# Neighbourhood attention on one core: values written to DRAM by SP's queue, scores and values interleaved in sets of three

## The chip, the cores and the metric

One Trainium2 chip, one of its cores. The engines are TensorE (PE; PEld is its weight load), VectorE (DVE), ScalarE (ACT), GpSimd (POOL) and SyncE (SP), each with its own instruction queue; SP computes nothing, it issues most of the DMAs. The metric is the device time of one execution in microseconds; all times below are microseconds. The kernel before took 715.81 in the median of three runs (713.94 to 717.45).

## The reference

Two blocks on an image batch x of shape 2 x 48 x 48 x 384, each with a group norm in front and a residual around it. The first, which the change touches, is 7 x 7 neighbourhood attention with 16 register tokens:

```python
qkv = gn(x) @ qkv_w.T + qkv_b                      # 12 heads of 32
reg_kv = registers @ qkv_w[384:].T + qkv_b[384:]   # 16 keys and values seen by every query
scores = einsum('bnqe,bnke->bnqk', q, concat(k, reg_k)) / sqrt(32)
scores = where(in_7x7_window_or_register, scores, -1e30)
o = einsum('bnqk,bnke->bnqe', softmax(scores), concat(v, reg_v))
x = x + o @ out_w.T + out_b
```

The second is a mixture of 4 experts, 2 of them chosen per token, of width 96. Matrix products are made in three float16 passes (high x high, high x low, low x high).

## The kernel before

There are six attention **stages** (`gi` 0 to 5): image `gi // 3`, and 4 of the 12 heads (128 channels). A stage works on six vertical **strips** of 8 columns by 48 rows (`s`, 384 tokens). Within a strip there are six **slots** of eight rows (`a`), so 36 steps n = 6s + a. Each stage has three parts.

*Opening.* Keys of the stage (six row blocks), which ScalarE and VectorE split into halves and SP writes to the DRAM scratch `kscr`; then per strip the queries, written to `qscr` by POOL (`queries_out`, L332), between them the output projection of the stage before (`project_out`, added into X by VectorE at L517). In stages 2 and 5, after the projection, `parameters` (VectorE) and `deviation` (ScalarE, with a change of activation table on each side) make the next group norm's scale, and TensorE waits for it (`gn_par`) before its next work. In stage 0 `value_bias` stands between the queries of strips 4 and 5, and TensorE waits for its result `obx` (L593) before the scores.

*Middle part.* It makes two things. First, the **scores for maxima** of strips 0, 1 and 2: `scores(gi, s, i)`, six units i of eight matmuls (L1002) each, each unit in one PSUM bank, each reduced by VectorE (`maximum`, L523). When the six are done, `split_maxima` splits them, `maxima_turned` on TensorE transposes them (L1012), ScalarE copies them (`maxima_out`, L776, semaphore `t_ev`), and POOL sends them into two rows of QS by DMA (`maxima_in`, L355). Second, the **values** of all six strips: `values(gi, s, b)`, 27 matmuls a strip, three for each of three channel blocks and three token blocks b, into the bank `V_BANK`. ScalarE copies a strip to `VT[:, s % 2]` (`values_out`, L770, semaphore `v_sb`). POOL writes it with three DMAs to `vscr` (`values_out`, L339, semaphores `v_out[s % 2]`). VT has two buffers, so ScalarE's copy of strip s waits until the write of strip s - 2 has landed. SP loads windows of `vscr` into VR (`values_in`, L255: six DMAs a strip, 14 columns of a slot each, semaphores `vr_in`), which waits for the writes of strips s and s + 1.

TensorE's order is: scores 0 (six units), values 0, values 1, turn maxima 0, scores 1, values 2, values 3, turn maxima 1, scores 2, values 4, values 5. ScalarE's: values 0, 1, maxima 0, values 2, 3, maxima 1, values 4, 5. POOL's: values 0, 1, register values, maxima 0, values 2, 3, maxima 1, values 4, 5.

*Steps.* 36 steps: `key_scores(gi, n)` (L1026, transposed scores less the maxima), ScalarE's exponentials (`exps`, L787, four buffers), and `weighted(gi, n)` (L1045, weighted values and sums), issued two steps behind. The scores of strips 3, 4 and 5 for their maxima are spread between them. `weighted(gi, 0)` waits for the first three transfers of VR. The scores of strip 4 stand behind step 13 and wait for its keys in the slot of strip 0 (`kb_in`).

**SP's queue** sets much of the order. For each stage, in program order:

```python
for s in range(4):
    keys_in(gi, s)        # KB slot s, 3 DMAs (L238), and a table (L235) for s of 0, 1
    queries_in(gi, s)     # waits for q_out of the strip, 3 DMAs (L244)
for s in (4, 5):
    queries_in(gi, s)
for s in (0, 1):
    values_in(gi, s)      # 6 DMAs each (L255)
# stage 4: load of fc1; stage 5: six small loads for the experts
for s in range(4):
    if s < 2:
        sp.wait_ge(s_["st_mm"], 36 * gi + 6 * (s + 1))
        keys_in(gi, s + 4)
    values_in(gi, s + 2)
```

A wait on SP holds everything behind it. Line numbers are those of the profile.

## Time and profile before

| | us |
|---|---|
| median of 3 runs (range) | 715.81 (713.94 to 717.45) |
| profiled execution, its own time | 715.22 |
| its span, first to last instruction | 713.3 |
| PE busy | 593.1 (83%) |
| PE weight loads busy | 413.9 (58%) |
| DVE busy | 474.6 (67%) |
| ACT busy | 296.3 (42%) |
| POOL busy | 300.5 (42%), 57.2 of it issuing `vscr<-VT` |
| mean granted TensorE clock | 0.962 of full |

The profile gives each instruction's start and duration, and for idle time of an engine before an instruction its releaser, the instruction or DMA whose semaphore came last. "x8" is eight instructions of one kind shown as one row; the duration is then from the first start to the last end. A DMA's duration in the trace is that of its issue; its landing is another number. The clock is the share of full speed that was granted.

### The profile page before, as it was taken

How to read it: one execution, taken by the hardware profiler on the slowest of the kernel's cores; microseconds unless marked ns; L12 is line 12 of the kernel's file. 1: busy time of each engine (PE TensorE's matmuls, PEld its weight loads, DVE VectorE, ACT ScalarE, POOL GpSimd, SP SyncE). 2: the span in 40 equal slices, each digit the busy share in tenths (PEclk: the TensorE clock that was granted, in tenths of full speed). 3: DMA queues.
4: the chain of work that ended last, by engine and by line, in shares of the span. 5: the costliest groups of instructions: out<-in, count | busy, mean ns of one | idle time of the engine just before them, and what ended most of it. 6: DMA issues, size and time to landing. Idle time of an engine off the chain costs nothing.

```text
span 713.3 us, 22313 instructions
## 1 busy us (share of the span) xinstructions
PE 593.1 (83%) x9225; PEld 413.9 (58%) x9225; DVE 474.6 (67%) x1024; ACT 296.3 (42%) x586; POOL 300.5 (42%) x437
## 2 busy tenths in 40 slices
PE   0686899988997887987898878988777786799997
PEld 0433777667764765566765767557555443455554
DVE  3784566777976699774866768866797476652332
ACT  2343355315632377313552246323584226533231
POOL 4312789235221745318872532216454025621331
PEclk9997999999999999999999989999899898899999
DMA  8959751895359641694429772596520000001102
GB/s 322 277 152 219 203 131 46 215 252 149 92 126 238 187 114 45 164 263 135 123 72 256 209 174 59 123 240 177 152 57 2 1 33 34 34 34 67 66 36 99
DMA packets 130940, 95.93 MB, mean 134 GB/s; under 512 B 67340, under 2 KB 125384, under 8 KB 130072
## 3 DMA queue, kind: packets, MB, share of 16 engines
q1 hardware_dynamic: 121960, 78.72, 42.5%
q0 software_dynamic: 8880, 15.79, 7.4%
q8 instruction: 73, 1.20, 0.7%
q14 instruction: 27, 0.22, 0.1%
HBM read 58.11 MB, written 35.54 MB: 131 GB/s over the span
## 4 chain that ended last, share of the span: by engine, by line
PE 42%; DVE 20%; DMA 15%; ACT 7%; issue 7%; POOL 5%; SPq 3%; ACTq 0%; DVEq 0%; POOLq 0%
PE ps L904 25%; PE ps L1045 6%; DMA qscr<-QT 5%; DMA vscr<-VT 4%; DVE MX L523 4%; PE ps L1026 4%; PE ps L1002 4%; POOL vscr L339 3%; DMA KB<-kscr 2%; DVE GT_ L466 2%; DMA X<-in_x 2%; DVE ST L434 2%; DVE X L517 1%; ACT KB L734 1%; DVE KT L501 1%
## 5 line engine op out<-in xcount | busy, mean ns | idle before, releaser
L523 DVE TENSOR_REDUCE MX<-ps 128x2 f32<-128x456 f32 x216 | 124.4, 626 | 63.3 <-PE ps L1002 62.3
L904 PE MATMUL ps<-XH,WQ 128*128 128x384 f16 x810 | 151.6, 344 | 13.9 <-DVE XH L473 6.4
L904 PEld LDWEIGHTS ps<-XH,WQ 128*128 128x128 f16 x810 | 80.9, 102 | 76.7 <-issue 21.4
L787 ACT ACTIVATE PT<-ps 128x448 f32<-128x448 f32 (+1 forms) x162 | 79.0, 510 | 58.8 <-PE ps L1026 57.7
L1002 PE MATMUL ps<-KB,QS 120*32 120x228 f16 x1728 | 66.1, 276 | 31.9 <-DVE MX L523 9.9
L1026 PE MATMUL ps<-QS,KB 122*128 122x112 f16 (+1 forms) x864 | 65.6, 215 | 17.2 <-ACT VT L770 7.0
L339 POOL DMA_DIRECT2D vscr<-VT x108 | 57.2, 537 | 50.3 <-ACT VT L770 45.9
L409 POOL TENSOR_TENSOR OS<-QS,OS 128x384 f16<-128x384 f32 x36 | 32.3, 912 | 101.6 <-ACT OS L879 101.6
L904 PE MATMUL ps<-OS,WO 128*128 128x384 f16 x324 | 62.4, 343 | 13.3 <-DVE X L517 12.0
L332 POOL DMA_DIRECT2D qscr<-QT x36 | 26.3, 732 | 108.8 <-DVE QT L507 108.8
L1026 PEld LDWEIGHTS ps<-QS,KB 122*128 122x128 f16 x864 | 44.3, 100 | 38.4 <-ACT PT L787 13.0
L904 PE MATMUL ps<-OS,WQ 128*128 128x384 f16 x324 | 61.1, 336 | 6.4 <-POOL KB L317 4.3
L1002 PEld LDWEIGHTS ps<-KB,QS 120*32 120x32 f16 x1728 | 38.0, 99 | 46.4 <-DVE MX L523 14.7
L355 POOL DMA_DIRECT2D QS<-MT x72 | 38.2, 537 | 61.4 <-ACT MT L776 61.2
L1045 PE MATMUL ps<-PT,VR 128*32 128x112 f32 (+1 forms) x1296 | 61.7, 264 | 1.1 <-issue 0.8
L904 PE MATMUL ps<-WQ,XH 128*128 128x128 f16 x972 | 59.6, 223 | 0.8 <-issue 0.8
L1045 PE MATMUL ps<-PT,ONE 128*32 128x112 f32 (+1 forms) x1296 | 59.5, 258 | 0.0
L904 PEld LDWEIGHTS ps<-WQ,XH 128*128 128x128 f16 x972 | 56.2, 100 | 4.7 <-issue 4.7
L675 DVE TENSOR_TENSOR QS<-ps,QS 128x384 f32<-128x384 f32 x36 | 19.6, 554 | 53.6 <-POOL OS L409 27.7
L904 PEld LDWEIGHTS ps<-OS,WO 128*128 128x128 f16 x324 | 32.2, 102 | 39.4 <-issue 18.9
L517 DVE SCALAR_TENSOR_TENSOR X<-ps,X 128x384 f32<-128x384 f32 x108 | 53.0, 549 | 2.0 <-PE ps L904 1.2
L770 ACT ACTIVATE VT<-ps 128x384 f32<-128x384 f32 x36 | 17.7, 490 | 87.7 <-PE ps L904 55.4
(159 smaller groups left out, 978.7 us busy)
## 6 DMA issues: line engine op xcount, KB each, us to landing
KB<-kscr SPq DMA_DIRECT2D x108, 192.0 KB, 7.0
kscr<-KT SPq DMA_DIRECT2D x72, 192.0 KB, 2.5
VR<-vscr SPq DMA_DIRECT2D x216, 56.0 KB
QS<-qscr SPq DMA_DIRECT2D x108, 96.0 KB, 5.6
X<-in_x SPq DMA_DIRECT2D x6, 1152.0 KB, 18.9
qscr<-QT POOLq DMA_DIRECT2D x36, 192.0 KB, 5.1
vscr<-VT POOLq DMA_DIRECT2D x108, 64.0 KB, 2.3
out<-X SPq DMA_DIRECT2D x12, 576.0 KB, 3.3
```

The lines of the kernel that those rows point to most:

```text
L332: pool.dma_start(qscr.rearrange("a p n -> p a n")[:, :, s * SN:(s + 1) * SN], QT[:, s % 2, :, :]).then_inc(q_out[s % 2], 16)
L339: pool.dma_start(vscr[16 * b:16 * b + 16, CT_ * s + 3:CT_ * s + 3 + CT_, :], VT[:, s % 2, b, :]).then_inc(v_out[s % 2], 16)
L355: pool.dma_start(QS[SROWS + part:SROWS + part + 1, :, s * SN:(s + 1) * SN], MT[part * HEADS:(part + 1) * HEADS, s % 2, :]).then_inc(m_in[s ...
L409: nc.gpsimd.tensor_tensor(HW[:, m % 2, 1, k, :], HF[:, unit % 2, :], HW[:, m % 2, 0, k, :], ALU.subtract).then_inc(s_["hl"], 1)
L517: V.scalar_tensor_tensor(out=xj, in0=ps[:, OP_BANK(gi, s, j), 0:SN], scalar=1 / WS, in1=xj, op0=ALU.mult, op1=ALU.add).then_inc(s_["op_don ...
L523: V.tensor_reduce(out=MX[:, s % 2, t, 2 * pair:2 * pair + 2], in_=ps[:, S_BANK(s, i), 0:2 * RUN].rearrange("p (h n) -> p h n", h=2), op=AL ...
L675: V.tensor_tensor(HF[:, unit % 2, :], ps[:, 2 + k, 0:SN], GE[:, unit % 2, :], ALU.mult).then_inc(s_["hf"], 1)
L787: A(PTS[n % 4][:, 0:w], ps[:, ST_BANK(n), 0:w], ACT.Exp, scale=SCORE).then_inc(s_["exd"], 1)
L904: last = mm(bank, lhsT(a, k), rhs(b, k), start=(k == 0 and n == 0), stop=(finish and k == steps - 1 and n == 2))
L1002: last = mm(ps[32 * j:32 * j + 32, S_BANK(s, i), hh * RUN:(hh + 1) * RUN], QS[0:SROWS, h, q0:q0 + 32], KB[0:SROWS, h, slot(s), CHUNK * a:C ...
L1026: last = mm(ps[:, ST_BANK(n), h * w:(h + 1) * w], KB[0:TROWS, h, slot(s), LEAD + CHUNK * a:LEAD + CHUNK * (a + 1)], QS[0:TROWS, h, s * SN ...
L1045: last = mm(ps[DH * h:DH * (h + 1), bank, CT_ * q0:CT_ * q1], lhsT, PTS[n % 4][:, h * w:(h + 1) * w], start=(a == 0), stop=(a == STRIPS - ...
```

## The change

1. **Value writes.** `values_out` moves from POOL's queue to SP's, behind `queries_in` of strips 4 and 5 and ahead of `values_in` of strips 0 and 1. SP so writes all six strips of values before it loads any. POOL keeps `register_values` and `maxima_in`, now directly after its query writes.
2. **Order on TensorE.** `three_scores(k)` makes half a strip's scores. In stages 1 to 5: three scores, then a strip of values, six times, with the maxima of strip 0 turned after the fourth set and those of strip 1 after the sixth. In stage 0: values 0, 1, 2, value bias, and then three scores and a strip of values until both are used up.
3. **ScalarE.** Maxima 0 are copied after values 2 and maxima 1 after values 4; in stage 0 both after values 5.
4. **Banks.** The turned maxima use bank 0 throughout (was 7 or 1), values 5 use bank 1 in stages 1 to 5, the bias uses 7. Scores of strip 2 now wait for the maxima copy of strip 0 (`t_ev`), scores of strip 3 for all values copies. The first two `key_scores` wait for values copy 4 (stages 1 to 5) in place of 4 and 5.
5. **Parameters.** In stages 2 and 5 `deviation` and `parameters` stand after the queries of strip 3 in place of after the projection.

```diff
-        V_BANK = (2, 3, 2, 3, 2, 3)
+        V_BANK = lambda gi, s: 1 if gi and s == TILES - 1 else 2 + s % 2
-        S_BANK = lambda s, i: (0, 1, 4, 6, 5, 7)[i] if s < 3 else i % 2
+        S_BANK = lambda s, i: (0, 1, 4, 6, 5, 7)[i] if s < 3 else (i + 1) % 2
-        T_BANK = lambda s: 7 if s < 2 else 1
...
     # SP
+            def values_out(gi, s):
+                sp.wait_ge(s_["v_sb"], 6 * gi + s + 1)
+                if 36 * gi > 0:
+                    sp.wait_ge(s_["pv"], 36 * gi)
+                for b in range(KC):
+                    sp.dma_start(vscr[16 * b:16 * b + 16, CT_ * s + 3:CT_ * s + 3 + CT_, :], VT[:, s % 2, b, :]).then_inc(v_out[s % 2], 16)
...
                 for s in (4, 5):
                     queries_in(gi, s)
+                for s in range(TILES):
+                    values_out(gi, s)
                 for s in (0, 1):
                     values_in(gi, s)
...
     # POOL (its values_out, the same with pool for sp, goes)
-                for s in range(TILES):
-                    values_out(gi, s)
-                    if s == 1:
-                        register_values(gi)
-                    if s in (1, 3):
-                        maxima_in(gi, s // 2)
+                register_values(gi)
+                for s in (0, 1):
+                    maxima_in(gi, s)
...
     # VectorE
-                    if gi == 0 and s == 5:
-                        (obx)
                     if gi and s:
                         projected(gi - 1, s - 1)
+                    if gi in (2, 5) and s == 3:
+                        parameters(gi // KC + 1, 0)
                 if gi:
                     projected(gi - 1, TILES - 1)
-                if gi in (2, 5):
-                    parameters(gi // KC + 1, 0)
                 for s in range(3):
                     for i in range(6):
                         maximum(gi, s, i)
+                        if gi == 0 and s == 0 and i == 2:
+                            (obx)
...
     # ScalarE
-                if gi in (2, 5):
-                    deviation(gi // KC + 1)
-                    A(cols["warm"], cols["ob"][:, 0:1], ACT.Exp)
+                    if gi in (2, 5) and s == 3:
+                        deviation(gi // KC + 1)
+                        A(cols["warm"], cols["ob"][:, 0:1], ACT.Exp)
                 for s in range(TILES):
                     values_out(gi, s)
-                    if s in (1, 3):
-                        maxima_out(gi, s // 2)
+                    if gi and s in (2, 4):
+                        maxima_out(gi, s // 2 - 1)
+                if gi == 0:
+                    for s in (0, 1):
+                        maxima_out(gi, s)
...
     # TensorE, values: before strip 5's
+                    elif gi and s == TILES - 1:
+                        pe.wait_ge(s_["mx"], 36 * gi + 14)
     # scores
-                if i == 5 and s in (1, 2) or i == 1 and s >= 3:
+                if i == 0 and s == 2:
+                    pe.wait_ge(s_["t_ev"], 6 * gi + 1)
+                if i == 0 and s == 3:
+                    pe.wait_ge(s_["v_sb"], 6 * gi + 6)
+                if i == 1 and s >= 3:
                     pe.wait_ge(s_["t_ev"], 6 * gi + s)
     # key_scores
-                    pe.wait_ge(s_["v_sb"], 6 * gi + n + 5)
+                    pe.wait_ge(s_["v_sb"], 6 * gi + (5 if gi else 6))
     # order
-                for s in range(TILES):
-                    if s % 2 == 0:
-                        if s:
-                            maxima_turned(gi, s // 2 - 1)
-                        for i in range(6):
-                            scores(gi, s // 2, i)
-                    for b in range(KC):
-                        values(gi, s, b)
+                def three_scores(k):
+                    for i in range(3):
+                        scores(gi, k // 2, 3 * (k % 2) + i)
+                    if k in (3, 5):
+                        maxima_turned(gi, k // 2 - 1)
...
+                if gi == 0:
+                    for s in range(3):
+                        all_values(s)
+                    value_bias()
+                for k in range(6):
+                    three_scores(k)
+                    if gi:
+                        all_values(k)
+                    elif k < 3:
+                        all_values(3 + k)
```

## Rows read from the trace of the kernel before

**Rows 1.** The page, part 4: the chain that ended last, by engine.
```profile
PE 42%; DVE 20%; DMA 15%; ACT 7%; issue 7%; POOL 5%; SPq 3%; ACTq 0%; DVEq 0%; POOLq 0%
```

**Rows 2.** Waits of SP's queue: waiter, releaser, us in total, times, longest.
```profile
SPq L244 <- DMA qscr<-QT: 30.1, 12, 4.4
```

**Rows 3.** Timeline of stage 1's middle part: start, us, engine, line, what, count.
```profile
149.62 1.35 PE L1002 MATMUL ps<-KB,QS 120*32 120x228 f16 x48
150.91 3.19 PE L904 MATMUL ps<-WQ,XH 128*128 128x128 f16 x54
...
152.63 0.49 ACT L770 ACTIVATE VT<-ps 128x384 f32<-128x384 f32 x1 [5.82 <-PE ps L904]
...
153.42 3.16 POOL L339 DMA_DIRECT2D vscr<-VT  x6 [4.93 <-ACT VT L770]
...
159.77 0.49 ACT L770 ACTIVATE VT<-ps 128x384 f32<-128x384 f32 x1 [4.80 <-DMA vscr<-VT]
...
160.60 8.43 SPq L255 DMA_DIRECT2D VR<-vscr  x12
...
167.88 0.36 PE L1045 MATMUL ps<-PT,VR 128*32 128x88 f32 x8
```

**Rows 4.** Timeline of SP: last query loads of stages 0, 1 and 5.
```profile
67.85 11.20 SPq L244 DMA_DIRECT2D QS<-qscr  x9
...
148.26 9.42 SPq L244 DMA_DIRECT2D QS<-qscr  x9
...
476.62 8.84 SPq L244 DMA_DIRECT2D QS<-qscr  x9
```

**Rows 5.** Line L244, SP's query loads: issue in ns, and landing.
```profile
L244 SPq DMA_DIRECT2D QS<-qscr x108: 302/433/1649, 58.4 to 484.1; - x108
...
DMA to landing us min/median/max: 2.4/5.6/8.9
```

**Rows 6.** Line L339, POOL's value writes: landing.
```profile
DMA to landing us min/median/max: 1.9/2.3/5.2
```

**Rows 7.** Line L230, SP's key writes `kscr<-KT`: landing.
```profile
DMA to landing us min/median/max: 2.4/2.5/6.9
```

**Rows 8.** Busy time by stretch: A:B, us, each engine, granted clock, DMA share, GB/s.
```profile
149.60:164.90 15.30, 13.84 (x314) 12.62 (x314) 11.59 (x26) 3.15 (x7) 9.58 (x19) 1.00 0.84 215
422.60:427.60 5.00, 4.92 (x100) 4.05 (x104) 3.37 (x7) 0.98 (x2) 0.00 (x0) 0.50 0.52 109
```

**Rows 9.** Timeline of PE: first scores of strip 4, stages 0, 1, 4, 5.
```profile
98.91 0.57 PE L1002 MATMUL ps<-KB,QS 120*32 120x228 f16 x16
...
175.96 0.57 PE L1002 MATMUL ps<-KB,QS 120*32 120x228 f16 x16
...
422.68 0.95 PE L1002 MATMUL ps<-KB,QS 120*32 120x228 f16 x16 [3.04 <-DMA KB<-kscr]
...
510.90 0.95 PE L1002 MATMUL ps<-KB,QS 120*32 120x228 f16 x16 [4.20 <-DMA KB<-kscr]
```

**Rows 10.** Timeline of SP: issues ahead of strip 4's keys, stages 4 and 5.
```profile
413.41 0.38 SPq L235 DMA_DIRECT2D KB<-in_ktab  x1
...
502.38 0.36 SPq L279 DMA_DIRECT2D KT<-in_fc  x1
...
504.67 0.32 SPq L235 DMA_DIRECT2D KB<-in_ktab  x1
```

**Rows 11.** Timeline of PE: first scores of stages 0 and 5.
```profile
69.69 2.47 PE L1002 MATMUL ps<-KB,QS 120*32 120x228 f16 x48 [2.97 <-DVE SM L593]
...
479.26 1.38 PE L1002 MATMUL ps<-KB,QS 120*32 120x228 f16 x48 [1.76 <-DVE SM L451]
```

**Rows 12.** Timeline of PE: first weighted sums, stages 0 and 5.
```profile
90.08 0.51 PE L1045 MATMUL ps<-PT,VR 128*32 128x88 f32 x8
...
497.83 0.36 PE L1045 MATMUL ps<-PT,VR 128*32 128x88 f32 x8
```

**Rows 13.** Line L238, SP's key loads `KB<-kscr`: landing.
```profile
DMA to landing us min/median/max: 5.2/7.0/8.9
```

More of the change, by code:

```diff
@@ L332, in queries_out @@
                 pool.dma_start(qscr.rearrange("a p n -> p a n")[:, :, s * SN:(s + 1) * SN], QT[:, s % 2, :, :]).then_inc(q_out[s % 2], 16)
-            def values_out(gi, s):
-                pool.wait_ge(s_["v_sb"], 6 * gi + s + 1)
-                if 36 * gi > 0:
-                    pool.wait_ge(s_["pv"], 36 * gi)
-                for b in range(KC):
-                    pool.dma_start(vscr[16 * b:16 * b + 16, CT_ * s + 3:CT_ * s + 3 + CT_, :], VT[:, s % 2, b, :]).then_inc(v_out[s % 2], 16)
             def register_values(gi):
@@ L603, in _ @@
                         maximum(gi, s, i)
+                        if gi == 0 and s == 0 and i == 2:
+                            dve.wait_ge(s_["bv_mm"], 1)
+                            V.scalar_tensor_tensor(out=cols["obx"], in0=ps[:, 7, 0:KC], scalar=1 / WS, in1=cols["ob"],
+                                                   op0=ALU.mult, op1=ALU.add).then_inc(s_["obx"], 1)
                     split_maxima(gi, s)
@@ L775, in maxima_out @@
                     act.wait_ge(m_in[s % 2], 96 * gi + 32 * (s // 2))
-                nc.scalar.copy(MT[:, s % 2, :], ps[0:2 * HEADS, T_BANK(s), 0:SN // 2].bitcast(F16)).then_inc(s_["t_ev"], 1)
+                nc.scalar.copy(MT[:, s % 2, :], ps[0:2 * HEADS, 0, 0:SN // 2].bitcast(F16)).then_inc(s_["t_ev"], 1)
             def exps(gi, n):
@@ L931, in value_bias @@
                 for j in range(KC):
-                    last = split_product(ps[:, 1, j:j + 1], lambda a, k: WO[:, a, k, j * P:(j + 1) * P], lambda b, k: BVH[:, b, k:k + 1])
+                    last = split_product(ps[:, 7, j:j + 1], lambda a, k: WO[:, a, k, j * P:(j + 1) * P], lambda b, k: BVH[:, b, k:k + 1])
                 last.then_inc(s_["bv_mm"], 1)
@@ L972, in values @@
                         pe.wait_ge(s_["q_lo"], 6 * gi + 5 + s)
+                    elif gi and s == TILES - 1:
+                        pe.wait_ge(s_["mx"], 36 * gi + 14)
                     else:
                         pe.wait_ge(s_["v_sb"], 6 * gi + s - 1)
-                last = split_product(ps[:, V_BANK[s], P * b:P * (b + 1)], lambda a, k: xh1(a, k, s * SN + b * P, P),
+                last = split_product(ps[:, V_BANK(gi, s), P * b:P * (b + 1)], lambda a, k: xh1(a, k, s * SN + b * P, P),
                                      lambda q, k: WQ[:, gi % KC, q, k, 2 * P:3 * P])
@@ L983, in scores @@
                     pe.wait_ge(qs_in[s], 48 * (gi + 1))
-                if i == 5 and s in (1, 2) or i == 1 and s >= 3:
+                if i == 0 and s == 2:
[3 more added lines that the diff above has]
+                if i == 1 and s >= 3:
                     pe.wait_ge(s_["t_ev"], 6 * gi + s)
+                if gi == 0 and s == 0 and i == 5:
+                    pe.wait_ge(s_["obx"], 1)
                 if s == 0:
@@ L1007, in maxima_turned @@
                 pe.wait_ge(s_["mxh"], 6 * gi + s + 1)
+                if s < 2:
+                    pe.wait_ge(s_["mx"], 36 * gi + 6 * s + 7)
                 if 6 * gi + s > 0:
                     pe.wait_ge(s_["t_ev"], 6 * gi + s)
-                bank = ps[0:2 * HEADS, T_BANK(s), 0:SN // 2].bitcast(F16)
+                bank = ps[0:2 * HEADS, 0, 0:SN // 2].bitcast(F16)
                 for t in range(3):
```

11 lines of the change are left out of this document (3 added, 8 removed).

## The prediction

> **What bounds the kernel now.** I read the page's chain first [rows 1]. TensorE leads it, but DMA, VectorE and issuing together hold a good third, so the six attention stages are chains of handovers more than sums of matmuls. Next came SP's own waits [rows 2]: before its loads of the last strips of queries it stood 30.1 us in 12 waits for the landing of `qscr<-QT`. Then stage 1 engine by engine [rows 3]. Its middle part begins at 149.62 with the scores of strip 0. A group of six score units takes 1.35, two strips of values take 3.19, ScalarE's copy of a strip of values 0.49. The third values copy starts only at 159.77, after 4.80 of waiting for the write of strip 0's values, because VT has two buffers. The values come back to SBUF from 160.60 (12 transfers, 8.43), and the first weighted sum starts at 167.88. So the middle part is timed by value writes, and its end by the reload of VR.
>
> **When SP is free.** Today POOL issues the write at 153.42, 0.3 after the copy. In the change SP does, after all query loads. SP ends those at 67.85 + 11.20 = 79.05 in stage 0, at 157.68 in stage 1, at 485.46 in stage 5 [rows 4] (first, second and last of six; their sum is 1682.1). Call that moment s. In stage 1 the first values are ready at 153.12, so their write is held for 4.6 us.
>
> **Price of one write on SP.** No row shows it. Issue: SP's nearest shapes take 0.43 (`QS<-qscr`) [rows 5] and, with the gap to the next, 0.70 (`VR<-vscr`, 8.43 over 12) [rows 3]; the first has as many runs, the second the same tensor, so I take 0.6 between them and keep both ends. Landing: the same write from POOL lands in 1.9 at best and 2.3 in the median [rows 6], SP's `kscr<-KT` in 2.4 and 2.5 [rows 7]; I take 2.2 and keep 1.9 to 2.5. The Trainium skill ("DMA: Bandwidth & Descriptors", section "Latency and other measured facts") gives SP's path a first byte some 0.4 us earlier than GpSimd's. The rows just named do not show that; by the rule the one such landing on the chain would save an estimated 0.4 a stage, 2.4 us in all, and the sum leaves it out.
>
> **The chain of a stage, from s.** Three issues and a landing: strip 0's values are written at 0.05 + 2 x 0.6 + 2.2 = s+3.45. ScalarE copies strip 2's values (s+4.0) and, next in its order, the first turned maxima, about as long (s+4.5). The scores of strip 2 now wait for those maxima. TensorE by then has done two thirds of its part: four sets of three scores and four strips of values, 9.2 us of work, at 158.8 in stage 1, and it stands until 162.3. What is left is two sets of three, two strips of values and a transpose: 0.6 + 1.6 + 0.6 + 0.2 + 1.6 = 4.6 [rows 3]. After idle times of 3 us and more the trace grants half the clock (0.50 behind the idle 3.04 of stage 4, against 1.00 in the middle part of stage 1) [rows 8], which is 1.2 GHz for 2.4, and two units of scores take 0.95 for 0.57 there [rows 9]; I add 2.0. With the last copy, strip 5's values are in VT at s+11.9. The writes of strips 1 to 4 are spent in between (each 1.8 of issue) and end nothing. SP then writes strip 5 (to s+13.85), and only then turns to VR, since `values_in(0)` is queued behind `values_out(5)`: third transfer at +1.4, landing 2.2, so the first weighted sum starts at s+17.5. In stage 1 that is 175.2 against 167.88 [rows 3], 7.3 late.
>
> **What is late next.** Behind the 12 VR transfers (8.4) come the keys of strip 4, at s+22.3. In stage 5 they went out at 504.67 and the scores that need them started at 510.90, after 4.20 of waiting for them alone: 6.2 [rows 9, 10]. So these scores start at s+28.5. In stage 1: 186.2, against 175.96, so 10.2 late; the weighted sums alone would have asked for them at 175.2 + 8.1 = 183.3. The keys therefore carry the delay, and the rest of the stage follows them as now, since it is the same work in the same order. Over six stages: the six s sum to 1682.1, plus 6 x 28.5 is 1853.1; the six starts now sum to 1810.0 (98.91, 175.96, 422.68 and 510.90 are four of them) [rows 9]: 43.1. Stage 4 has fc1 ahead of the keys and took 9.3 from their issue at 413.41 to the scores: 3.5 more, its own 0.46 of issue included. Stage 5 has six small loads there, 502.38 to 504.67: 2.3 more [rows 10]. Stage 0 turns no maxima before its last values and is 1.6 ahead of the template. Sum 47.3. In stages 0 to 3 the wait for keys is new, and if the half clock follows it for 3 us at the rate of those two units it costs 1.2; the wait is short, so half of that, 4 x 0.6 = 2.4, goes in. Together 49.7.
>
> **The other edits.** *Parameters among the queries* (stages 2 and 5) takes away the 1.76 that TensorE waited for them in stage 5 [rows 11] and shifts two table loads under the queries' DMA waits; but the part then ends by s, which waits on a landing that does not move, so it is worth 0 here, and 3.6 at most (twice 1.8) if SP were early. *First group opens with values*: the stage 0 scores waited 2.97 for the bias [rows 11]; the values can start some 4 us before 69.69. Strip 4's values then wait for strip 2's copy, hence for s: worth 0 again, 4 at most. The value bias moves into the same cover. *Scores in sets of three* lets VectorE's maxima run beside values and frees the second half of the banks in time; VectorE is not last in this part, so 0. *POOL without 108 issues* brings maxima in earlier, which nobody waits for first: 0. The bank changes cost nothing. Without SP's delay these would all count, which is the third and fourth case below.
>
> **Total.** The profiled execution took 715.2 (span 713.3 and 1.9 around it), 0.6 under the median of 715.8. 715.2 + 49.7 = 764.9.
>
> **Rivals.** *(A) The keys are in time.* If the keys of strip 4 land in 4 us rather than 6.2, only the first weighted sum is late: s+17.5 in each stage against its six starts now, 90.08 to 497.83 [rows 12], whose sum is 1751.5; 35.6, less 1.6 in stage 0, so 749. Against it: `KB<-kscr` never landed under 5.2 [rows 13]. *(B) The writes stand behind reads.* On SP they follow `QS<-qscr`, which took a median of 5.6 to land [rows 5]. If strip 0's write needs 5.6 rather than 2.2, each stage is 3.4 later: 785. For it: SP issues both, one behind the other. Against it: POOL's writes met the same reads at the same engines, and 2.3 was their median, with 5.2 the worst [rows 6]. *(C) No difference.* If the writes get out as the values come, TensorE's 14.1 of work bounds the part (3 x 1.35 + 3 x 3.19 and the turns): last copy at 14.6, strip 5's write 1.9, VR 3.6, first weighted sum 20.1 after the start. Now it is 19.1 on average of six, from 69.69 to 90.08 in stage 0 to 479.26 to 497.83 in stage 5 [rows 11, 12], so 6 us are lost, and the earlier openings give 7.6 back: 714. The Trainium skill ("Trainium Kernel Development and Optimization", section "Key Constraints") says that issuing from several engines saves the sequencer's issue time alone; taken by itself that is this case. It needs s some 5 us earlier, and SP's 30.1 us of waits speak against it [rows 2]. *(D) Faster.* As C, with issues of 0.3 (SP's shortest `QS<-qscr`) [rows 5] and landings of 1.9: first weighted sum at 18.1, so 702. It is decided by the same point, whether SP reaches the writes before VT's two buffers are full.
>
> **Chances and range.** The forecast 0.68, A 0.14, B 0.09, C 0.05, D 0.04. The bounds of the terms: issue 0.43, landing 1.9 and keys 5.2 take some 3 a stage (747); 0.69, 2.5 and keys at the median 7.0 add some 2.2 a stage (778). With the clock's share and most of A and B the range is 742 to 784. A time within 0.5% (3.6 us) of the old one can't be told from no change: faster 0.04, same 0.05, slower 0.91.
>
> **What would show it.** Right: SP's wait for `VT L770` before its value writes; strip 0's write starting within 0.1 of the last query load; ScalarE's third values copy later than now by 1 to 4; TensorE idle some 3.5 before the fifth set of scores, released by `MT L776`; TensorE idle before the first weighted sum with a DMA as releaser, and before strip 4's scores for `KB<-kscr` in all six stages. Wrong: VR's first transfer less than 12 after s (the writes are cheaper), the keys landed when asked for (A), or a landing of strip 0's write far over 2.5 (B). If the first values are written as they come, the argument falls at its first step.

## The result, and the profile after

The changed kernel took 764.32 in the median of four runs (762.78 to 769.04), beside 715.27 (713.94 to 717.45) for the kernel before on the same chip: 1.0716 times as long, 95% interval 1.0661 to 1.0772. Forecast were 764.9 and a range of 742 to 784. Some executions run slower as a whole; ratios and intervals, here and below, leave these out, while a median is that of all executions.

The page of the changed kernel: span, busy time by engine, and part 4, the chain by engine. Copies of values are now at L768, of maxima at L774, SP's query loads at L243, value writes at L251, VR loads at L261, key loads at L234 and L237.

```profile
span 767.1 us, 22314 instructions
...
PE 611.8 (80%) x9225; PEld 427.6 (56%) x9225; DVE 476.0 (62%) x1024; ACT 296.2 (39%) x586; POOL 243.7 (32%) x329
...
PE 34%; DMA 22%; DVE 16%; SPq 13%; issue 7%; ACT 5%; POOL 2%; ACTq 0%; DVEq 0%; POOLq 0%
```

The engines have the same work as before (POOL less by 56.8, the writes); PE's 18.7 more are the same matmuls at a mean granted clock of 0.925 for 0.962. What grew is the chain's share of SP's queue, from 3 to 13%, and of DMA, from 15 to 22% [rows 1].

Timeline of SP in stage 1, from its last query loads to strip 5's keys:

```profile
157.57 6.18 SPq L243 DMA_DIRECT2D QS<-qscr  x6
163.85 14.93 SPq L251 DMA_DIRECT2D vscr<-VT  x18
178.88 8.42 SPq L261 DMA_DIRECT2D VR<-vscr  x12
187.35 0.48 SPq L234 DMA_DIRECT2D KB<-in_ktab  x1
187.88 1.26 SPq L237 DMA_DIRECT2D KB<-kscr  x3
```

Here s is 163.75, and the writes begin 0.1 later. They hold the queue for 15: 18 issues of 0.6 are 10.8, the rest lies between them. A part of it is waits for ScalarE's copies, 5.4 in all six stages, which the merged row hides. SP's own waits name them:

```profile
SPq L251 <- ACT VT L768: 5.4, 9, 1.1
```

In rows 3 the VR loads began at 160.60, 2.9 after s; now they begin 15.1 after it, and the keys behind them move along.

Timeline of ScalarE in stage 1, strip 0's, strip 2's and strip 5's values and the first turned maxima:

```profile
159.01 0.49 ACT L768 ACTIVATE VT<-ps 128x384 f32<-128x384 f32 x1 [5.23 <-PE ps L905]
...
167.99 0.49 ACT L768 ACTIVATE VT<-ps 128x384 f32<-128x384 f32 x1 [6.17 <-DMA vscr<-VT]
168.37 0.45 ACT L774 COPY MT<-ps 8x384 f16<-8x384 f16 x1
...
174.71 0.49 ACT L768 ACTIVATE VT<-ps 128x384 f32<-128x384 f32 x1 [0.86 <-PE ps L905]
```

The first values lie ready at 159.50 and wait 4.35 until SP issues their write. Their write lands at 167.90, the third copy follows at once (s + 4.2), then the maxima. Timeline of PE: the fifth set of scores in stages 1 and 2, the first weighted sum of stage 1, and strip 4's scores in stages 1, 2, 4 and 5:

```profile
169.08 1.33 PE L1011 MATMUL ps<-KB,QS 120*32 120x228 f16 x24 [0.22 <-ACT MT L774]
...
182.91 0.52 PE L1056 MATMUL ps<-PT,VR 128*32 128x88 f32 x8 [6.00 <-DMA VR<-vscr]
...
193.10 0.57 PE L1011 MATMUL ps<-KB,QS 120*32 120x228 f16 x16 [0.46 <-DMA KB<-kscr]
...
259.91 1.33 PE L1011 MATMUL ps<-KB,QS 120*32 120x228 f16 x24 [3.50 <-ACT MT L774]
...
283.42 0.57 PE L1011 MATMUL ps<-KB,QS 120*32 120x228 f16 x16 [0.84 <-DMA KB<-kscr]
...
465.04 0.95 PE L1011 MATMUL ps<-KB,QS 120*32 120x228 f16 x16 [3.03 <-DMA KB<-kscr]
...
559.12 0.57 PE L1011 MATMUL ps<-KB,QS 120*32 120x228 f16 x16 [3.27 <-DMA KB<-kscr]
```

TensorE's longest new wait is the one before the first weighted sum. Two of the waits of all stages: waiter, releaser, total, times, longest:

```profile
ACT VT L768 <- DMA vscr<-VT: 66.4, 20, 9.6
...
PE ps L1056 <- DMA VR<-vscr: 25.5, 6, 6.0
```

The price of a write on SP, which no row of before had: line L251, issues in ns, and landing.

```profile
L251 SPq DMA_DIRECT2D vscr<-VT x108: 517/598/1751, 77.7 to 541.6; - x108
...
DMA to landing us min/median/max: 2.0/2.1/3.7
```

**Where the time went.** With a stage's end as the end of its last weighted sum, the six stages end at 120.9, 197.7, 285.0, 365.2, 446.2 and 538.9 before, and at 127.3, 214.7, 309.8, 397.3, 489.1 and 587.7 after: losses of 6.4, 10.6, 7.7, 7.4, 10.8 and 6.0, together 48.9. The medians differ by 49.0. The execution that was profiled took 769.04, the longest of the four; its other 5.0 lie behind the stages (179.4 for 174.4), where the change does nothing. That its six stages alone give the 49.0 of the medians is therefore in part chance: the other three executions have no trace here.

### The profile page after: what moved, and what is told of

It reads as the page before. It is cut to its first block, busy times and chain, and to the rows that moved or that the text cites. A ratio compares the mean times of both kernels' runs of the same rounds, so it can differ in the third digit from the quotient of the medians.

```text
span 767.1 us, 22314 instructions
## 1 busy us (share of the span) xinstructions
PE 611.8 (80%) x9225; PEld 427.6 (56%) x9225; DVE 476.0 (62%) x1024; ACT 296.2 (39%) x586; POOL 243.7 (32%) x329
## 4 chain that ended last, share of the span: by engine, by line
PE 34%; DMA 22%; DVE 16%; SPq 13%; issue 7%; ACT 5%; POOL 2%; ACTq 0%; DVEq 0%; POOLq 0%
PE ps L905 20%; DMA qscr<-QT 11%; SPq L261 6%; PE ps L1056 5%; DMA KB<-kscr 4%; DMA vscr<-VT 4%; SPq L251 3%; DVE MX L521 3%; PE ps L1037 3%; PE ps L1011 2%; DMA X<-in_x 2%; DVE GT_ L464 2%; DVE ST L432 2%; SPq L243 1%; SPq L237 1%
## 5 line engine op out<-in xcount | busy, mean ns | idle before, releaser
L905 PE MATMUL ps<-XH,WQ 128*128 128x384 f16 x810 | 148.4, 340 | 16.1 <-DVE XH L471 7.9
L1011 PE MATMUL ps<-KB,QS 120*32 120x228 f16 x1728 | 68.9, 280 | 36.8 <-DMA KB<-kscr 10.8
L1056 PE MATMUL ps<-PT,VR 128*32 128x112 f32 (+1 forms) x1296 | 64.6, 276 | 25.5 <-DMA VR<-vscr 25.5
L905 PE MATMUL ps<-WQ,XH 128*128 128x128 f16 x972 | 68.1, 234 | 11.7 <-ACT VT L768 5.1
L1037 PE MATMUL ps<-QS,KB 122*128 122x112 f16 (+1 forms) x864 | 66.6, 221 | 10.4 <-ACT PT L785 4.9
L905 PEld LDWEIGHTS ps<-WQ,XH 128*128 128x128 f16 x972 | 61.6, 106 | 18.6 <-issue 8.7
L905 PE MATMUL ps<-OS,WQ 128*128 128x384 f16 x324 | 64.1, 347 | 6.5 <-POOL KB L325 4.5
L1011 PEld LDWEIGHTS ps<-KB,QS 120*32 120x32 f16 x1728 | 36.1, 99 | 54.8 <-issue 22.2
L1037 PEld LDWEIGHTS ps<-QS,KB 122*128 122x128 f16 x864 | 46.2, 103 | 31.4 <-ACT PT L785 11.9
L1056 PE MATMUL ps<-PT,ONE 128*32 128x112 f32 (+1 forms) x1296 | 62.6, 269 | 0.0
L768 ACT ACTIVATE VT<-ps 128x384 f32<-128x384 f32 x36 | 17.6, 490 | 112.0 <-DMA vscr<-VT 66.4
L340 POOL DMA_DIRECT2D qscr<-QT x36 | 26.4, 733 | 107.3 <-DVE QT L505 107.3
L673 DVE TENSOR_TENSOR QS<-ps,QS 128x384 f32<-128x384 f32 x36 | 19.6, 555 | 55.3 <-POOL OS L407 28.4
L1056 PEld LDWEIGHTS ps<-PT,VR 128*32 128x32 f32 x1296 | 35.3, 118 | 31.8 <-issue 26.8
## 6 DMA issues: line engine op xcount, KB each, us to landing
X<-in_x SPq DMA_DIRECT2D x6, 1152.0 KB, 18.7
```

The lines of the kernel that those rows point to most:

```text
L340: pool.dma_start(qscr.rearrange("a p n -> p a n")[:, :, s * SN:(s + 1) * SN], QT[:, s % 2, :, :]).then_inc(q_out[s % 2], 16)
L905: last = mm(bank, lhsT(a, k), rhs(b, k), start=(k == 0 and n == 0), stop=(finish and k == steps - 1 and n == 2))
L1011: last = mm(ps[32 * j:32 * j + 32, S_BANK(s, i), hh * RUN:(hh + 1) * RUN], QS[0:SROWS, h, q0:q0 + 32], KB[0:SROWS, h, slot(s), CHUNK * a:C ...
L1037: last = mm(ps[:, ST_BANK(n), h * w:(h + 1) * w], KB[0:TROWS, h, slot(s), LEAD + CHUNK * a:LEAD + CHUNK * (a + 1)], QS[0:TROWS, h, s * SN ...
L1056: last = mm(ps[DH * h:DH * (h + 1), bank, CT_ * q0:CT_ * q1], lhsT, PTS[n % 4][:, h * w:(h + 1) * w], start=(a == 0), stop=(a == STRIPS - ...
```

## Experiments

The last column holds means over the six stages, counted from s, the end of SP's last query load, all read off the traces: strip 0's write landed, ScalarE's copy of strip 5's values done, first VR load issued, first weighted sum, strip 4's keys issued, strip 4's scores begun. From there to the stage's end every kernel takes 23.7 to 24.2.

| kernel | us | landed, copy 5, VR, sum, keys, scores |
|---|---|---|
| before | 715.3 | 1.7, 9.5, 3.0, 11.6, 14.2, 21.3 |
| after | 764.3 | 4.0, 11.6, 14.3, 18.6, 23.5, 29.5 |
| E1 writes on POOL, new order | 716.15 | 1.9, 10.1, 3.1, 13.0, 15.2, 22.0 |
| E2 writes on SP, old order | 767.07 | 4.8, 12.8, 15.4, 19.6, 24.6, 30.7 |
| E3 two writes ahead of strip 5's queries | 758.55 | VR 11.1, sum 15.4, keys 20.3, scores 26.4 |
| E4 VR of strip 0 ahead of writes 4, 5 | 760.28 | VR 9.5, sum 14.8, keys 23.2, scores 29.2 |
| E5 parameters alone | 710.62 | 1.8, 9.4, 3.2, 11.4, 13.8, 20.5 |
| E6 writes on ScalarE, new order | 744.51 | 1.8, 12.0, 3.0, 16.9, 19.1, 25.6 |
| E8 writes on ScalarE, old order | 768.05 | copy 16.5, VR 3.8, sum 20.7, keys 22.9, scores 29.9 |
| E9 before, 18 spare issues a stage | 757.74 | 2.6, 10.2, 13.3, 17.3, 22.5, 28.8 |
| E12 before, 9 spare issues a stage | 728.08 | 1.9, 10.3, 7.1, 12.9, 17.0, 23.0 |
| E10 after, VR loads of strips 0, 1 on POOL | 732.30 | 4.0, 11.9, 7.6, 14.8, 17.5, 24.2 |
| E11 before, parameters and seven loads moved | 704.13 | 1.4, 9.4, 2.8, 11.4, 13.0, 19.3 |
| E13 before, seven loads moved | 706.27 | 2.3, 9.6, 3.6, 11.7, 13.5, 20.0 |

E2, E3, E4, E9 and E12 are one execution each. Those of the changed kernel range over 6.3, so the totals of E2, E3 and E4 can't be told from its own; there the times after s speak. E12's total is rough for the same reason: it lies 7 above the slowest of the 11 executions of the kernel before that were measured beside it (710.23 to 721.33). In E3 a part of the writes stands ahead of s, so its times after s are shorter by that alone.

**E1: the whole change, but the writes stay on POOL.**

```diff
     # SP
-                for s in range(TILES):
-                    values_out(gi, s)
     # POOL
+                for s in range(TILES):
+                    values_out(gi, s)
+                    if s == 1:
+                        register_values(gi)
+                    if gi and s in (2, 4):
+                        maxima_in(gi, s // 2 - 1)
...
```

> The changed kernel with one thing undone: POOL issues the value writes again, each as soon as ScalarE's copy is done; all else (the order in sets of three, banks, parameters among the queries) stays. Theory (SP's late writes carry the whole loss): the write of strip 0 starts 0.3 after its copy, VR loads start about 11 after the middle part's first scores, strip 4's keys go out about 19.5 after them, and the time falls to 697 to 708, under the 715 of the kernel before, because the other edits now count. Rival (the new order costs by itself, by the waits on the turned maxima and the freed banks): the time stays over 720 with POOL's writes too. Second rival (the other edits are worth nothing in either case): 714 to 717.

Measured 716.15 (713.68 to 719.26) against 715.43, ratio 1.0048 (1.0010 to 1.0085). So the new queue carries nearly all of the loss, 48 of 49, and the new order on TensorE brings nothing; by the ratio it costs half a per cent. The theory's 697 to 708, a gain of 7 to 18 by the order and the other edits, was wrong; the second rival, 714 to 717, held. Stage 1 of E1, on POOL, ScalarE and PE: strip 0's write, the third copy, the maxima behind it, the fifth set of scores.

```profile
154.74 1.61 POOL L338 DMA_DIRECT2D vscr<-VT  x3 [4.34 <-ACT VT L772]
...
161.89 0.49 ACT L772 ACTIVATE VT<-ps 128x384 f32<-128x384 f32 x1 [5.13 <-DMA vscr<-VT]
162.27 0.45 ACT L778 COPY MT<-ps 8x384 f16<-8x384 f16 x1
...
162.98 0.77 PE L1015 MATMUL ps<-KB,QS 120*32 120x228 f16 x24 [0.64 <-ACT MT L778]
```

The write goes out at once, but in the midst of the query reads it takes 7.1 from its first issue to its landing, and the third copy waits for that as it did in rows 3 (where 153.42 to 159.77 is 6.3). As means of six stages the landing takes 6.8 here, 5.1 in the kernel before and 3.9 in the changed one. An order that makes values earlier on TensorE meets the same landing, and now scores also wait for the maxima behind the copy. In stage 0 both maxima copies stand behind strip 5's values, and the first transposed scores start at 90.35 instead of 84.48.

**E2: the kernel before, and only the writes on SP.**

```diff
     # SP (values_out as in the change; POOL's goes)
                 for s in (4, 5):
                     queries_in(gi, s)
+                for s in range(TILES):
+                    values_out(gi, s)
                 for s in (0, 1):
                     values_in(gi, s)
```

> The kernel before with one thing done: the value writes go to SP's queue at the place of the change; TensorE's order is the old one (six scores, two strips of values). Theory: the loss is in the queue, so this alone gives 752 to 762; slightly less than the change, as the last values copy needs one set of scores less behind the first maxima. Rival (the loss needs the new order): under 730.

Measured 767.07, above the bracket and within the range of the changed kernel: the loss needs nothing of the new order, and the order saves nothing that shows.

**E9 and E12: issue time by itself.** The kernel before, POOL's writes untouched, and at the place of SP's value writes 18 (E12: 9) transfers of the same shape from G, a constant tile of the norm, into a scratch that nobody reads.

```diff
+            def spare_out(gi, s):
+                for b in range(KC):
+                    sp.dma_start(spare[gi * TILES + s, ...], G[:, b, 0:P])
...
+                for s in range(TILES):        # E12: range(3)
+                    spare_out(gi, s)
```

> The kernel before, with POOL's value writes and the old order, and on SP, at the place of the change, 18 further writes a stage of the same shape from a constant tile to a spare DRAM tensor, which wait for nothing and nobody waits for. It measures the issue time by itself. Theory (SP's issues carry a good half of the loss, the rest is its waits for copies and their landings): VR loads start 12 after the last query load, against 1 to 5 now, strip 4's keys some 20 after it, and the time is 740 to 748. Rival A (issue alone is all): 760 and more. Rival B (issue is cheap, the waits for copies are all): under 725.

Measured 757.74, above the theory's 740 to 748 and just under rival A's 760: more of the loss is issue time than the theory gave it. Timeline of SP in its stage 1, and then the spare line, issues in ns:

```profile
155.31 9.21 SPq L246 DMA_DIRECT2D QS<-qscr  x9
164.57 12.74 SPq L263 DMA_DIRECT2D spare<-G  x18
177.77 8.44 SPq L257 DMA_DIRECT2D VR<-vscr  x12
```

```profile
L263 SPq DMA_DIRECT2D spare<-G x108: 537/602/2076, 77.9 to 534.3; - x108
```

No value waits for these transfers, strip 5's copy moves by 0.7 alone, and still 42.5 of the 49 are there (44.3 against the 713.48 of the kernel before measured beside it): they are 18 issues of 0.6 with their gaps (12.74 over 18 is 0.71) ahead of VR and the keys.

> The kernel before with 9 spare writes a stage on SP in place of 18. With 18, VR loads started 13.2 after the last query load against 3.0 now, strip 4's keys 22 after it, and the time rose by 43. Theory (the loss is SP's issue time, 0.67 a write, less the 3 that SP now waits anyway): half the writes start VR at 6.6 to 7, some 4 later than now, and cost 20 to 26: 734 to 740. Rival (it is the traffic at the DMA engines): with half of the bytes half of the loss and the same VR start as now; or, if any write in that place is enough, still 40.

Measured 728.08, under the 734 to 740 forecast: 12.8 more than before, not half of E9's. VR starts 4.1 later, as the theory had it; by the rival, the traffic, it would not have moved, and the spare writes do not hold up the keys' own transfers either (`KB<-kscr` lands in a median of 7.1 in E9, 7.0 before). Nine issues are 6.4 a stage, and the 3.0 in which SP stood before its VR loads anyway take up much of them: the keys go out 2.8 late and strip 4's scores begin 1.7 late. The second nine find no such slack and cost 29.7.

**E4: the VR loads of strip 0 ahead of the writes of strips 4 and 5.**

```diff
-                for s in range(TILES):
+                for s in range(4):
                     values_out(gi, s)
-                for s in (0, 1):
-                    values_in(gi, s)
+                values_in(gi, 0)
+                for s in (4, 5):
+                    values_out(gi, s)
+                values_in(gi, 1)
```

> The changed kernel with VR's loads of strip 0 moved on SP ahead of the writes of strips 4 and 5. SP's work is the same, but it no longer waits for the last copies. Theory (strip 4's keys carry the delay, by SP's total of issues): the first weighted sum comes 5 earlier in a stage, the keys only 2.5, and the time falls by 2 to 3 a stage, to 746 to 752. Rival (the first weighted sum carries it): 5 a stage, about 734. Second rival (neither; the copies are what is last): within 3 of the changed kernel.

Measured 760.28, 4.0 under the changed kernel, where the theory had 746 to 752 and the keys 2.5 earlier: its size failed. The times after s tell the two waits apart: the first weighted sum comes 3.8 earlier, the keys 0.3, the scores 0.3. So the keys carry the delay, as forecast: all 30 transfers are ahead of them in any order, and what the first weighted sum wins is lost again before strip 4's scores.

**E3: the writes of strips 0 and 1 ahead of strip 5's query loads.**

```diff
-                for s in (4, 5):
-                    queries_in(gi, s)
+                queries_in(gi, 4)
                 for s in range(TILES):
                     values_out(gi, s)
+                    if s == 1:
+                        queries_in(gi, 5)
```

> The changed kernel with the writes of strips 0 and 1 ahead of the loads of strip 5's queries on SP, so that they needn't wait for the landing of those queries. They start as soon as ScalarE has copied them, 4 to 5 earlier. Theory A (a write lands about 2.2 after its issue whatever reads stand before it): the third copy comes 4 earlier, and the time falls by some 4 a stage, to 738 to 742. Theory B (on SP the writes land behind the key and query loads issued before them, which took 7.0 and 5.6): they land 5 and more after their issue, and the gain is 1 to 2 a stage, 752 to 758.

Measured 758.55, half a microsecond above theory B's 752 to 758 and far from theory A's. Timeline of its stage 1, SP and ScalarE's third copy:

```profile
157.05 4.11 SPq L251 DMA_DIRECT2D vscr<-VT  x6
161.21 2.26 SPq L243 DMA_DIRECT2D QS<-qscr  x3
...
165.75 0.49 ACT L769 ACTIVATE VT<-ps 128x384 f32<-128x384 f32 x1 [6.41 <-DMA vscr<-VT]
...
166.27 10.25 SPq L251 DMA_DIRECT2D vscr<-VT  x12
```

Counted from the stage's first scores (154.12 here, 156.59 in the changed kernel), the write goes out after 2.9 in place of 7.3, and the third copy starts after 11.6 in place of 11.4. Strip 0's write landed at 165.67, 8.6 after its first issue, against 4.05 (163.85 to 167.90) when it was issued behind the last query load. Stage 1 is the extreme: the means of six stages are 6.4 and 3.9. What is gained in issue is lost in landing; the VR loads come 3.2 sooner after s because six writes are past by then, but these put s itself back.

**E6 and E8: the writes on ScalarE's queue,** each right behind its copy, in the new (E6) and the old order (E8).

```diff
     # ScalarE, values_out
+                for b in range(KC):
+                    act.dma_start(vscr[...], VT[:, s % 2, b, :]).then_inc(v_out[s % 2], 16)
```

> The changed kernel with the value writes issued by ScalarE's queue, each behind its own copy, instead of SP's. SP goes straight from the queries to the reloads. Theory (the place in the queue decides, not which kind of queue): the time falls back to that of the kernel before or a little under it, 705 to 718. Rival (three issues of 0.6 behind each copy hold up ScalarE's next copies, the turned maxima and the exponentials, and so TensorE): 725 and more.

Measured 744.51, ratio 1.0463 (1.0394 to 1.0531): the theory (705 to 718) failed and the rival held. Timeline of ScalarE in its stage 1:

```profile
163.31 0.49 ACT L759 ACTIVATE VT<-ps 128x384 f32<-128x384 f32 x1 [3.07 <-DMA vscr<-VT]
163.83 1.82 ACTq L764 DMA_DIRECT2D vscr<-VT  x3
165.75 0.47 ACT L770 COPY MT<-ps 8x384 f16<-8x384 f16 x1 [1.95 <-issue]
166.12 0.47 ACT L759 ACTIVATE VT<-ps 128x384 f32<-128x384 f32 x1
166.63 2.44 ACTq L764 DMA_DIRECT2D vscr<-VT  x3
```

SP is free (VR loads at s + 3.0, as before), yet three issues of 1.8 stand between a copy and the next one, and the maxima behind them. The first weighted sum comes 5.3 late: in this stage the exponentials ahead of it start only when strip 5's three issues are over, at 174.84.

> The kernel before with the value writes on ScalarE's queue, in the old order of TensorE. The maxima of strip 1 are copied behind two more writes here. Theory: 708 to 718, as with ScalarE's writes in the new order, within 5 of it. Rival (the new order is what uses free writes): 5 or more over the new order's time.

Measured 768.05, ratio 1.0762 (1.0710 to 1.0814), far from the 708 to 718. Against E6 the new order is worth 23.5 here: it spreads the copies, strip 5's ends at s + 12.0 instead of 16.5. On TensorE, in stage 1 of E8, the last unit of scores of strips 1 and 2 stands until the maxima of the strip before are copied, and each of these copies stands behind the issues of two strips on ScalarE:

```profile
166.25 0.57 PE L997 MATMUL ps<-KB,QS 120*32 120x228 f16 x8 [3.19 <-ACT MT L771]
...
175.12 0.38 PE L997 MATMUL ps<-KB,QS 120*32 120x228 f16 x8 [2.76 <-ACT MT L771]
```

Over all stages TensorE waits 30.8 for such copies in E8 and 16.6 in E6, 14.2 of the 23.5.

**E10: the changed kernel with the VR loads of strips 0 and 1 on POOL,** which SP so never issues.

```diff
     # SP
-                for s in (0, 1):
-                    values_in(gi, s)
     # POOL
-                for s in (0, 1):
-                    maxima_in(gi, s)
+                maxima_in(gi, 0)
+                values_in(gi, 0)
+                maxima_in(gi, 1)
+                values_in(gi, 1)
```

> The changed kernel, with SP's value writes kept and the 12 reloads of VR for strips 0 and 1 moved to POOL, which the change left idle. SP then goes from the writes straight to strip 4's keys. Theory (the sum of issues on SP ahead of strip 4's keys is what was lost): keys go out some 14 to 15 after the last query load in place of 23.5, the first weighted sum starts at 13 to 14 in place of 18.7, strip 4's scores at some 22 (21.3 now in the kernel before), and the time is 714 to 724. Rival (writes on SP are late by themselves, since VT's buffers wait for them): 735 and more.

Measured 732.30, ratio 1.0242 (1.0189 to 1.0294), between the 714 to 724 of the theory and the 735 of the rival: 32 of the 49 come back once 12 transfers (8.4 of issue) leave SP's queue. The keys were to go out 14 to 15 after s and went out at 17.5. SP was through with the writes at s + 14.2 and then, in stages 0 to 4, waited for TensorE to be done with strip 0's keys, whose slot they take (SP's own waits, L235 being the first load for that slot):

```profile
SPq L235 <- PE ps L1048: 13.7, 5, 6.2
```

So here the queue is no longer what is last. The other 17 stay with the writes: they still wait for s and follow one another on SP, strip 5's copy comes at s + 11.9 for 9.5, and the first weighted sum at s + 14.8 for 11.6. These 17 and the 42.5 of E9 are more than 49 together, since the two delays run side by side.

**E5: the kernel before, and only the parameters among the queries.**

> The kernel before with the parameters of the group norm among the queries in stages 2 and 5, and nothing else. In the changed kernel, and in the one with POOL's writes, the first scores of these two stages came 2.2 and 1.8 earlier after the end of the stage before. Theory (the prediction's 3.6 at most, if the writes go out as the values come): 711 to 714, ratio 0.994 to 0.999. Rival (the value writes behind it take it back, since their landing hangs on the queries' DMAs): no difference, 1.000.

Measured 710.62 against 713.48, ratio 0.9978 (0.9934 to 1.0021): no difference that these executions can tell from none, nor from the theory's 0.994 to 0.999.

**E11 and E13: a version that is faster than both.** Stages 4 and 5 of before lose 3.04 and 4.20 waiting for keys [rows 9] behind seven loads (fc1 in stage 4, six small ones in stage 5) that nobody needs for long [rows 10]. E13 moves these loads behind the keys; E11 does the same and moves the parameters as E5.

```diff
-                if gi == 4:
-                    sp.dma_start(wr_flat, fc1).then_inc(s_["f_in"], 16)
-                if gi == STAGES - 1:
-                    (wait for v_out, six small loads)
                 for s in range(4):
                     if s < 2:
                         sp.wait_ge(s_["st_mm"], 36 * gi + 6 * (s + 1))
                         keys_in(gi, s + 4)
+                    if gi == 4 and s == 1:
+                        sp.dma_start(wr_flat, fc1).then_inc(s_["f_in"], 16)
                     values_in(gi, s + 2)
+                    if gi == STAGES - 1 and s == 0:
+                        (wait for v_out, six small loads)
```

> A version to beat both: the kernel before, with the parameters among the queries and with the loads of fc1 (stage 4) and of the experts' small arrays (stage 5) behind strip 4's keys on SP, where they stood ahead of them. TensorE waited 3.0 and 4.2 for those keys in stages 4 and 5 of the kernel before. Theory: these waits go (6 to 7), and the parameters bring up to 4: 703 to 709, ratio 0.984 to 0.993. Rival (the keys' own landing or the reloads behind them take it back): ratio 0.995 and more.

> The kernel before with one edit: the loads of fc1's and the experts' arrays are queued behind strip 4's keys, not ahead of them; the parameters stay where they are. Theory A: the gain of the faster kernel that had both edits (704.1 us, ratio 0.988) is mostly this one; the waits for keys in stages 4 and 5 (3.0 and 4.2 us, and the half clock behind them) go, and the time is 706 to 710 us, ratio 0.988 to 0.994. Theory B: the gain needs the parameters' move as well (alone it gave 0.998), and this one alone gives 711 us or more, ratio 0.995 or above.

E11 took 704.13 against 715.24, ratio 0.9884 (0.9835 to 0.9933); E13 took 706.27 against 715.80, ratio 0.9881 (0.9841 to 0.9922), both as their theories had it. Strip 4's scores of stages 4 and 5 in E13, on PE:

```profile
417.39 0.57 PE L1002 MATMUL ps<-KB,QS 120*32 120x228 f16 x16
...
499.62 0.57 PE L1002 MATMUL ps<-KB,QS 120*32 120x228 f16 x16
```

Both waits and both half clocks of rows 9 are gone. The two stages take 76.35 and 88.01 instead of 81.01 and 92.70, 4.7 less each, together 9.35 of the 10.4 between the two traces. The moved loads alone make the gain, 1.2%, with intervals clear of 1; the parameters add nothing that shows.

Issue time is not all that moved. In stage 5 the six loads took 2.3 of SP's queue, and in front of them SP waited 3.1 for the landing of the last value writes (SP's waits in the kernel before):

```profile
SPq L277 <- DMA vscr<-VT: 3.1, 1, 3.1
```

In stage 4 fc1 took 0.46 of the queue only. But it is 576 KB, and the keys issued behind it were awaited 9.3 after their issue, where in E13, without it, the scores start 6.4 after it and wait for nothing. That points to the transfer itself and not to its issue, but no run separates the two.

## Why the prediction was right, point by point

| after s, mean of six stages | forecast | measured |
|---|---|---|
| strip 0's write landed | 3.45 | 4.0 |
| strip 5's copy done | 11.9 | 11.6 |
| VR loads begin | 13.9 | 14.3 |
| first weighted sum | 17.5 | 18.6 |
| strip 4's keys issued | 22.5 | 23.5 |
| strip 4's scores | 29.2 | 29.5 |
| from there to the stage's end | 24.4 | 24.1 |

(The last three forecasts are the means that follow from the template with its terms for single stages: the keys' 22.3 with stage 0's -1.6, stage 4's own 0.46 and stage 5's 2.3 spread over six; the scores' 28.5 with -1.6, 3.5 and 2.3; and the 24.0 of before with the clock's 2.4. The others are the template alone.)

**When SP is free** held: strip 0's write starts 0.1 after the last query load in five stages and 0.04 after it in stage 0. It is the step on which all stood, and the time between the values' being ready and their write (4.35 in stage 1, forecast 4.6) is never won back. Of the signs that were named one came weakly: SP's waits for copies before its value writes are 5.4 in nine waits over all stages, the longest 1.1, and none is before strip 0's.

**Price of a write.** 0.598 of issue for 0.6, 2.1 of landing for 2.2. The 0.5 that the first landing is later than forecast is mostly issue: from the first to the third issue SP took 1.6 on average for the 1.2 forecast, as in stages 1, 4 and 5 the second one held it for 0.9 to 1.6. The third transfer then landed in 2.3 on average; only stage 2's 3.6 is a trace of rival B, which asked for 5.6. The same write lands in a median of 2.1 from SP and 2.3 from POOL [rows 6]. With the rule that the Trainium skill states ("DMA: Bandwidth & Descriptors", section "Latency and other measured facts"; a first byte some 0.4 earlier from SP) the trace agrees in sign, with half the size. But the two stand at different places among the reads, and in E9, in one kernel, SP's spare writes of the same shape landed in a median of 2.5 and POOL's writes in 2.3, so no run shows a lead of SP's path by itself.

**The chain.** Copy, write and bank waits came as foretold: the third values copy started 4.1 after s for 1.9 before, and TensorE stood before the fifth set 3.5 and 3.3 in stages 2 and 3 with the maxima copy as releaser, 2.15 in stage 5. In stages 1 and 4 it stood 1.95 and 2.37 somewhat earlier, in the midst of values and of scores, with nothing in the profile to name as releaser, and had less to wait for later; the copies were not moved by that. Strip 5's copy came at 11.6, and that is also what the forecast's own terms add up to: 4.5 to the maxima copy, 4.6 of work, 2.0 for the half clock and 0.5 for the copy; the text has 11.9. The 2.0 was too much. Half the clock came there in stages 2 and 3, behind the idle 3.5 and 3.3: from the fifth set to the end of the last values TensorE took 6.2 and 6.4, against 4.9 in stage 5, where 2.15 idle was followed by the full clock, and 5.6 in stage 1. Stages 1 to 3 so lost 0.7 to 1.6.

**What is late next.** The keys carried the delay (E4), with a wait in all six stages: 0.49, 0.46, 0.84, 0.83, 3.03, 3.27. In stages 0 to 3 it was shorter than the 2.9 of the argument (186.2 less 183.3), since TensorE asked later. The first weighted sum was itself 1.1 later than forecast (from the first VR load to that sum it took 4.3 for 3.6), and from that sum to asking for strip 4's scores TensorE took 9.0 to 9.7 in these stages, where the forecast took stage 1's 8.1. Two delays of nearly equal length run beside each other, and the later one counts.

**The clock's term was mis-sized and misplaced.** For stages 0 to 3 the sum held 2.4, if half the clock followed the new waits for keys. It did not: two units of scores take 0.57 in all four, and from strip 4's scores to the stage's end all six lose 0.7 together. It followed the longer wait before the first weighted sum instead. Stretches of 5 us of the changed kernel, the first from the first weighted sum of stage 1, the second from strip 4's scores of stage 5; the third number from the end is the granted clock:

```profile
182.90:187.90 5.00, 4.99 (x88) 4.04 (x88) 1.56 (x3) 1.11 (x3) 0.00 (x0) 0.51 0.30 86
559.12:564.12 5.00, 4.93 (x120) 3.80 (x120) 4.15 (x9) 1.57 (x3) 0.92 (x1) 0.66 0.65 166
```

Behind the idle 6.00 of stage 1 TensorE was granted 0.51, where the kernel before has 1.00, and its first eight matmuls took 0.52 for 0.36 [rows 3]. From the first weighted sum to asking for strip 4's scores it took 9.4 on average for 8.5. This ran while the keys were under way, so it shortened the wait for them and cost next to nothing. In stages 4 and 5 half the clock followed the wait for keys as it had before: at once in stage 4 (0.95 after 3.03 idle), and in stage 5 a little later (0.57 after 3.27 idle, then 0.95 for two units at 562.19). The length of the idle time alone does not tell when the half clock comes: in E4 it came behind 2.19 (0.95, stage 2), in E9 not at once behind 3.93 (0.57, stage 4).

The sum of what was measured: 8.2 a stage to the scores, 49.2, and 0.7 behind them, 49.8 in all, less 1.0 by which the stages' openings were shorter: 48.9. The forecast was 47.3 + 2.4 = 49.7. That it came within 1 is in part luck: the 1.9 that the steps were too short and the 1.7 that the clock's term was too long cancel. The openings' 1.0 was not foreseen, and need not be the change's: stage 0's s alone came 1.4 earlier, at 77.68, and in the kernels whose stage 0 opens as before it lies anywhere from 77.4 to 79.1.

**The other edits** were put at nothing. The parameters: first scores in stages 2 and 5 come 2.1 and 1.8 sooner after the end of the stage before, but s after the same end moves by -0.6 and 0.0, so what TensorE gains it gives back before SP. E1 tells it for all of them together: with SP's delay taken away they do not gain either. The text said that then "these would all count", toward 714 by case C or 702 by case D; E1's 716 is C's result, and D's gain is nowhere.

**Rivals.** A needed keys that land in 4. From their issue to the scores it took 6.0 on average. B needed landings of 5.6; the median was 2.1. Its mechanism exists all the same: in E3, with three query loads still to be issued behind them, the first three transfers of stage 1 landed 6.4 to 7.4 after their issue. In the change the writes stand behind all of the loads' issues. C needed SP at the writes some 5 us earlier, and the first of them went out 0.1 after s in every stage. E9 gives the size of what it left out: 108 issues of 0.6 that another queue had carried for nothing put 42.5 on the chain. Case C's own number for the new order with POOL's writes, 20.1 from the stage's first scores to the first weighted sum, is near E1's 19.8. The Trainium skill ("Trainium Kernel Development and Optimization", section "Key Constraints") says that issuing from several engines saves the sequencer's issue time alone; the runs agree, and that time alone was nearly the whole difference here.

## What to carry to other kernels

Before a transfer is moved to another queue, list all that stands behind its new place and ask when each is needed: 18 issues of 0.6 ahead of loads that are needed soon are 10.8 us a stage, and 12.7 with the gaps between them (E9), less the time the queue stood idle there anyway. What the transfers themselves take can come on top if they are large, as it seems for fc1. The same list read the other way found the gain: seven loads not needed for long, and a wait, stood ahead of keys that were waited for, and moving them behind the keys was worth 1.2%. A freer order on TensorE gained nothing here (E1): ScalarE's third copy still waited for its buffer, 5.13 in stage 1 for 4.80 before.

## What was not expected of the hardware

A write that is issued among query reads, with more of them to be issued behind it, lands later than one issued behind the last of them. From its first issue to the landing of its third transfer strip 0's write took 8.6 from SP in E3 and 7.1 from POOL in E1 in stage 1, against 4.05 in the changed kernel; over six stages it is 4.8 to 8.6 (mean 6.4), 5.7 to 7.6 (6.8) and 3.3 to 4.8 (3.9). POOL's and SP's queue both show it. The reads need not have landed for it: in stage 1 of the changed kernel the last of them landed at 167.29, 3.4 after the write's first issue. What makes the difference, no run separates. And a transfer issued by ScalarE occupies it like work: 0.62 in the median (L764 of E6, 0.525 to 1.852), so the three of a strip (1.82 to 2.44 in the rows of E6) hold ScalarE at least 3.7 times as long as the copy that they follow (0.49).
